# Mixture layer: the turned gates and the bias table padded from 9 to 128 rows

## The reference, cut to what matters

```python
logits = xf @ gate_w                                   # 8 experts
top_logits, top_idx = jax.lax.top_k(logits, K)         # K = 2
top_gates = jax.nn.softmax(top_logits, axis=-1)
gates = sum over k of one_hot(top_idx, E) * top_gates
h = gelu(einsum('nd,edh->neh', xf, w1) + b1)
out_e = einsum('neh,ehd->ned', h, w2) + b2
routed = einsum('ne,ned->nd', gates, out_e)
shared = gelu(xf @ shared_w1 + shared_b1) @ shared_w2 + shared_b2
return routed + shared
```

## Time and profile before

| | us |
|---|---|
| median of three timed runs | 1104.35 |
| lowest, highest | 1102.13, 1109.96 |
| the profiled execution, its own time | 1109.56 |
| its span in the trace | 1107.8 |
| TensorE matmul busy | 1027.1 (93%) |
| VectorE busy | 734.4 (66%) |
| ScalarE, GpSimd busy | 380.8, 225.1 |
| mixture phase, from its first product to the span's end | 936.7 to 1107.8 |

### The profile page before, as it was taken

The page is one execution under the profiler, slowest core; times in us unless marked ns, Lnnn a source line. Parts: engine busy times, 40 slices in busy tenths (PEclk is TensorE's granted clock), DMA queues, the critical chain, the costliest instruction groups (busy, mean ns, idle before and its releaser), DMA issues. The chain is left out here.

```text
span 1107.8 us, 16580 instructions
## 1 busy us (share of the span) xinstructions
PE 1027.1 (93%) x5736; PEld 856.1 (77%) x5736; DVE 734.4 (66%) x1657; ACT 380.8 (34%) x731; POOL 225.1 (20%) x284
## 2 busy tenths in 40 slices
PE   6799999999999999998699999688999986999998
PEld 5688888888888888887588888577777875877775
DVE  7666667666666676665669775667778874366456
ACT  4343433333434333333142321034554442322220
POOL 2222222222222222221100001221222224011011
PEclk9999999999999999999999999989999997899999
DMA  9300000000000000000120000020000000000000
GB/s 304 105 1 0 0 0 0 0 0 0 0 0 0 0 0 0 0 1 20 58 70 1 1 0 1 11 85 1 0 0 0 1 1 1 1 15 15 10 20 19
DMA packets 19033, 20.56 MB, mean 19 GB/s; under 512 B 4905, under 2 KB 14898, under 8 KB 18994
## 3 DMA queue, kind: packets, MB, share of 16 engines
q1 hardware_dynamic: 18994, 20.05, 5.5%
HBM read 17.95 MB, written 2.10 MB: 18 GB/s over the span
## 5 line engine op out<-in xcount | busy, mean ns | idle before, releaser
L393 POOL TENSOR_TENSOR rope_sum<-rope_cos,rope_sin 128x512 f32<-128x512 f32 x80 | 113.1, 1414 | 262.4 <-DVE rope_sin L514 262.4
L429 ACT ACTIVATE rope_exp<-rope_sum 128x512 f32<-128x512 f32 x80 | 50.5, 631 | 213.1 <-POOL rope_sum L393 213.0
L783 PE MATMUL proj<-wo_sb,attn_out_t 128*128 128x256 f32 x512 | 113.2, 379 | 0.7 <-issue 0.7
L783 PEld LDWEIGHTS proj<-wo_sb,attn_out_t 128*128 128x128 f32 x512 | 96.1, 190 | 13.4 <-issue 0.9
L732 PE MATMUL num<-v_ones,score_masked 128*128 128x129 f32 x512 | 100.2, 278 | 5.9 <-DVE score_masked L572 5.9
L1754 DVE SCALAR_TENSOR_TENSOR m_acc<-m_expert,gates,m_acc 128x256 f32<-128x256 f32 x128 | 61.9, 484 | 58.4 <-PE m_expert L1833 52.2
L733 PE MATMUL num<-state,q_t 128*128 128x129 f32 x512 | 99.8, 277 | 0.0
L511 DVE TENSOR_TENSOR rope_cos<-proj,cos_sb 128x512 f32<-128x512 f32 x80 | 55.3, 691 | 57.5 <-PE proj L686 57.5
L732 PEld LDWEIGHTS num<-v_ones,score_masked 128*128 128x128 f32 x512 | 83.0, 193 | 13.4 <-DVE score_masked L572 8.0
L1554 PE MATMUL g_ps<-t_u,k_rows 128*128 128x128 f32 x512 | 72.5, 284 | 16.6 <-DVE t_u L1403 16.4
L1554 PEld LDWEIGHTS g_ps<-t_u,k_rows 128*128 128x128 f32 x512 | 63.3, 191 | 30.2 <-DVE t_u L1403 27.8
(11 more groups left out here) (205 smaller groups left out, 2006.6 us busy)
## 6 DMA issues: line engine op xcount, KB each, us to landing
a_stage<-in_wqkv SPq DMA_DIRECT2D x6, 512.0 KB, 5.2
wo_sb<-in_wo SPq DMA_DIRECT2D x1, 2048.0 KB, 9.8
a_stage<-in_wgu SPq DMA_DIRECT2D x4, 512.0 KB, 8.5
out<-x_sb SPq DMA_DIRECT2D x16, 128.0 KB, 1.7
x_sb<-in_x SPq DMA_DIRECT2D x2, 768.0 KB, 11.2
f_wmod<-in_wmod SPq DMA_DIRECT2D x1, 1536.0 KB, 9.3
w_sb<-in_w SPq DMA_DIRECT2D x1, 1280.0 KB
a_wmod<-in_wmod SPq DMA_DIRECT2D x1, 1024.0 KB, 6.1
```

What stands on the lines that cost most here:

```text
L393: pool.tensor_tensor(y[:, parity], t1[:, parity], t2[:, parity], ALU.add).then_inc(s["y_done"], 1)
L783: mm = pe.matmul(proj[:, b, 0:D], o_t[:, i, :], wo[:, i, :], start=(i == 0), stop=(i == H - 1))
```

## The change

The gates array gets 128 columns instead of 9, filled with zeros and with ones in column 8; its turned form gets 128 rows; the bias table gets 128 rows, filled with zeros by GpSimd before its 9 rows are loaded. So the product at line 1819 is 128 rows deep, as those around it; rows 9 to 127 add zeros. The fill of the table makes SyncE's DMA of b2 wait for the second `zeroed` signal, and the two fills of the gates take one step of the `gate_step` count.

```diff
-            ... ("b2_sb", [E + 1, D]) ...
+            ... ("b2_sb", [P, D]) ...
@@ scan_phase, SyncE
-                sp.dma_start(b2[:], a["b2"]).then_inc(self.moe_in, 16)
+                sp.wait_ge(zeroed, 2)
+                sp.dma_start(b2[0:E + 1, :], a["b2"]).then_inc(self.moe_in, 16)
@@ scan_phase, GpSimd
                 pool.memset(k_diag[:], 0.0).then_inc(zeroed, 1)
+                pool.memset(self.moe_small[2][:], 0.0).then_inc(zeroed, 1)
@@ moe_phase
-            gates = sb("gates", [P, 2, GT, E + 1])
-            gates_t = sb("gates_t", [E + 1, 2, GT, P])
+            gates = sb("gates", [P, 2, GT, P])
+            gates_t = sb("gates_t", [P, 2, GT, P])
@@ gates_turned, ScalarE
-                    act.activation(gates_t[:, g % 2], small[0:E + 1, :].rearrange(...), ACT.Copy
+                    act.activation(gates_t[:, g % 2], small[:].rearrange(...), ACT.Copy
@@ gating, VectorE
-                    base = 6 * g
+                    base = 1 + 6 * g
@@ VectorE, start of the phase
-                dve.memset(gates[:], 1.0)
+                dve.memset(gates[:], 0.0).then_inc(s["gate_step"], 1)
+                dve.wait_ge(s["gate_step"], 1)
+                dve.memset(gates[:, :, :, E:E + 1], 1.0)
@@ gates_turn, TensorE
-                        t = pe.transpose(small[0:E + 1, i * P:(i + 1) * P], gates[:, g % 2, i, :], ident[:])
+                        t = pe.transpose(small[:, i * P:(i + 1) * P], gates[:, g % 2, i, :], ident[:])
```

More of the change, by code:

```diff
@@ L1120, in scan_phase @@
         self.moe_small = [self.keep.enter_context(nc.sbuf_tensor(n, shape, F32)) for n, shape in (
-            ("w2_sb", [P, NH, D]), ("b1_sb", [P, NH]), ("b2_sb", [E + 1, D]), ("gate_w_sb", [P, KD, E]))]
+            ("w2_sb", [P, NH, D]), ("b1_sb", [P, NH]), ("b2_sb", [P, D]), ("gate_w_sb", [P, KD, E]))]
         with ExitStack() as ctx:
@@ L1678, in gates_turned @@
                     act.wait_ge(s["gturn_full"], g + 1)
-                    act.activation(gates_t[:, g % 2], small[0:E + 1, :].rearrange("p (i t) -> p i t", i=GT), ACT.Copy
+                    act.activation(gates_t[:, g % 2], small[:].rearrange("p (i t) -> p i t", i=GT), ACT.Copy
                                    ).then_inc(s["gturn_done"], 1)
```

## The result

The changed kernel took 1102.23 us (median of 11 runs, 1098.97 to 1105.64); the kernel before, run beside it, 1107.49 us (11 runs, 1102.13 to 1111.78). The ratio is **0.9946, 95% interval 0.9926 to 0.9966**: 6.0 us faster, between 3.8 and 8.2. (The ratio is the middle one of all pairs of a run after and a run before; the two medians are 5.3 us apart.) That is the forecast's size and its class (within 1%). The median of before had been 1104.35 on the first three runs; with eleven it is 3.1 us higher, so the predicted 1098.8 is low by about as much (3.4 us), but the measured time is inside the range.

What follows compares the result with a forecast made beforehand. TensorE, busy 93% of the span, was taken as the bound, losing time around the bias products. From the median, 1104.35 - 5.85 (depth) + 0.2 (fill) = 1098.7; forecast 1098.8 us, range 1093.5 to 1104.

Steps and rivals of the forecast that it cites:

- Which gaps, and that they go: Idle "issue" time before the loads of the bias product and line 1821 falls from 5.4 and 6.1 to under 1 us each.
- upper bound of 10.6 us: Most that padding the bias product could gain if every gap counts: the two idle totals, 5.3 + 5.3 us.
- The rival with only the way out: Gap into the bias product stays as cost of its waits; only 13 exits gain, 3.1 us; 1101.5 us, chance 0.09.
- Their size: One bias product costs 0.32 us going in plus 0.235 coming out, about 0.545 us more than a full-depth one.
- the full-depth pace is 1.54 / 8 = 0.1925 us each: Pace of full-depth TensorE instructions, taken from eight expert instructions between 1030.52 and 1032.06; used to size the gaps.
- The other signs: A group's period falls by about 1.3 us; VectorE's wait in the last group from 1.08 to about 0.5 us.
- Which tiles count: Tiles 0, 2, 3 beside hidden blocks and all four of the last group are on the chain; sum 5.85 us.
- nothing to gain on the way in: At tile 0 of every group, behind the logits, only the way out gains, 0.235 us each, 0.94 us in all.
- The clock: Three falls to half clock behind the logits vanish: 5.04 us from the profiled execution, not counted against the median.
- Rival 1: The clock goes on falling behind the logits; the profiled execution goes to 1103.9 us; chance 0.17.
- The fills and SyncE: Bias table's fill may hold VectorE's cast at the scan's start, +0.2 us; the mixture's fills and SyncE's later DMA cost 0.
- The rival that speaks for no gain: Depth is not the cause: gaps at the bias product stay, padding adds loads and fills; 1105.4 us, chance 0.06.

Runs made afterwards that it cites:

- d9: The changed kernel with all its wide tiles and fills, but the bias product reads only 9 rows again; 1105.85 us, ratio to the kernel before 0.9994.
- logits2: The changed kernel with the logits' products done twice over, 16 more short instructions per group; 1116.57 us.

## Why the prediction was right, point by point

**Which gaps, and that they go: right.** The idle time under "issue" on both sides of the bias product belonged to its depth, and went with it (d9 has it back to the tenth of a microsecond), but for the 1.1 us of the wait for the turned gates. The prediction took that wait for part of the gap, so its upper bound of 10.6 us was 9.5. The rival with only the way out was wrong: the load behind the hidden products is on time now, 0.23 us behind the one before.

**Their size: right in kind, too large by over a third.** The step that failed is "the full-depth pace is 1.54 / 8 = 0.1925 us each". The loads show 0.216. With it the padded stretch is 0.23 + 6 x 0.216 = 1.53 us and not 1.385, and a bias product saves 0.40 and not 0.545; the chain shows 0.39. The way out is 0.62 - 0.43 = 0.19 us late by this pace, and not 0.235. Together with the 0.32 of the way in that would be 0.51, but the four loads behind it take 0.76 us instead of 0.86, which gives 0.10 back. The other signs moved with the size: a group's period fell by 1.07 us where 1.3 was forecast, and VectorE's wait in the last group to 0.69 where about 0.5 was.

**Which tiles count: right.** Tile 1's gap was covered by the gating, the others not, and all four of the last group were on the path. Measured by the chain: 1.07 us per group beside hidden blocks (tile 0 0.29, tiles 2 and 3 0.39 each; reckoned 0.235 + 2 x 0.545 = 1.325). At tile 0 the prediction had "nothing to gain on the way in"; there was 0.10 us, since the bias load starts 0.21 us behind the last of the logits' loads, and 0.11 in the changed kernel. Then come three times 0.38 in the last group and 0.20 in its first tile (0.67 + 1.06 to 0.67 + 0.86). Sum: 3 x 1.07 + 3 x 0.38 + 0.20 = **4.55 us**, against 5.85.

**The clock: right for the profiled execution, not settled for the median.** All three falls are gone: 3 x 1.68 = 5.04 us. With the 4.55 that gives 9.6 us for the mixture. The traces have 171.1 us from its first product to the end before, and 161.7 after, 9.4 less. The remaining 1.2 us of the 10.6 between the spans lie ahead of the mixture. Between the timed runs the difference is 6.0 us (3.8 to 8.2): the depth's 4.55 and about 1.5 more, within what falls in some of the runs of before would give. That share is argued, not shown, and the interval holds 4.55 without it. I had counted none of it against the median, and the depth term was 1.3 us too large; that the forecast gain of 5.65 us comes so near to 6.0 is in part luck. Rival 1, that the clock goes on falling, was wrong for the full-depth kernel; but logits2 shows that it was near.

**The fills and SyncE: 0.2 us was put down, and it comes in some executions only.** The cast at the scan's start was not held any longer in nine of 11 executions, and 0.25 us longer in two; the fill of the gates was covered by VectorE's idle time to the amount reckoned (1.0 of 1.1 us). The ratio of d9, 0.9994 (0.9972 to 1.0017), bounds all of them together, the wide transposes and the later DMAs too, unless fewer falls of the clock hide a cost (d9's profiled execution has one, that of before three).

**The rival that speaks for no gain:** the Trainium skill's "TensorE: Matmul & The Clock Gate" says, in "Why this matters for your kernels", that a product of 32 rows takes as long as one of 128. By the loads' lengths (182 to 190 ns at 9 to 128 rows) the runs agree. By the time that it costs between full products they do not: 0.39 us more at 9, 32 and 64 rows alike.

## What to carry to other kernels

A small product between large ones is not cheap for being small. If its contraction is 64 rows or fewer and its neighbours' is 128, try padding its operands with zeros to over 64 rows, where the padding can be zeroed once and off the path; here, with fp32 products of 256 columns, that was worth 0.4 us for each such product on the critical chain. Where kinds of product change, read TensorE's pace from the starts of the weight loads, and check on the chain which of the gaps count before multiplying.

## What the runs showed of the hardware that was not expected

- The cost of a shallow product is a step between 64 and 65 rows: 1.59 us for the six instructions at 9, 32 and 64 rows, 1.29 to 1.30 us at 65, 96 and 128 (fp32, 256 columns, between products 128 rows deep; one execution each at 32, 64, 65 and 96).
- In 13 profiled executions a shallow bias product (0.29 us longer in a group's first tile) went together with the granted clock falling to half behind 16 short products: at least one fall in each of six with it (12 of their 18 places), none in seven without. That the gap itself brings the fall is not shown. A fall cost 1.68 us, nearly six times what the gap did. Doubling the short products brought it back (half clock in all three groups).
- A fill on GpSimd that starts while VectorE's cast is held took 0.46 us for 256 columns, where the long fill before it ran at 3.94 / 4608 x 256 = 0.22 us; the cast's own length, 1.76 us, was the same as without the second fill. So it was in nine of the 11 executions with this fill; in the other two the cast took 2.01 us and the fill 0.31.
